# A decoder layer with routed experts: the routing weights' store on another queue, gathers one step earlier, and the first two expert tiles interleaved with shared products

## The chip, the core and the metric

The kernel runs on one core of one Trainium2 chip. TensorE (PE) multiplies; VectorE (DVE), ScalarE (ACT) and GpSimd (POOL) do the elementwise work; SyncE (SP) mostly issues transfers. ACT and POOL can issue transfers too. Each engine works through its own list of instructions in order and waits on semaphores for the others; a transfer counts its semaphore up by 16 when it has landed. The metric is the device time of one execution in microseconds (us).

## What is computed

The layer has three parts: self attention with layer norm, a slot attention with a GRU and layer norm, and a feed forward part with a shared network and eight routed experts, two per token. The change lies in the third:

```python
router_probs = softmax(einsum('bsd,de->bse', x, gate_w) + gate_b)
expert_values, expert_indices = top_k(router_probs, k=2)
expert_values = expert_values / (sum(expert_values) + 1e-09)
h = gelu(einsum('bsd,edi->bsei', x, ew1) + eb1)
all_outputs = einsum('bsei,eid->bsed', h, ew2) + eb2
moe_out = einsum('bse,bsed->bsd', weights_E, all_outputs)   # weights_E: the two values per token
return x + _mlp(x, sh_w1, sh_b1, sh_w2, sh_b2) + moe_out     # then a layer norm
```

There are T = 2048 tokens of D = 256 numbers; the hidden size is I = 1024.

## The kernel before

**Shared network.** The tokens are cut into NG = 4 groups of 512. The hidden units are cut into IC = 8 parts of 128, so there are MS = 32 steps m (group m // 8, part m % 8). A step has an up product (6 matmuls of 512 columns), a gelu and a cast to fp16 on ACT (`hidden`), the low half of the split (value minus its fp16 cast) on POOL (`hidden_low` in `ffn_pool`), and a down product (12 matmuls of 256 columns). Every operand is split in a high and a low fp16 part, which gives three matmuls (`HILO`) for one product. PE takes up(m), then down(m - 2). The first MF = 24 steps run before the experts; the last eight after them, as work for the end.

**Routing**, on DVE beside that: `choose_experts` (two experts per token), `count_tokens` and `place_rows` (where each token's row goes), four `part_choices`, each followed by small matmuls `rows_of` on PE, then `name_rows` (the list `dst` of rows for every tile; semaphore `r_line` reaches `NAMED`) and `name_tiles` (each tile's expert, `TILES_KNOWN`). `weigh_choices` computes the two weights per token, `top_w`; `w_line` counts to 7 when they are there.

**The tokens for the experts** go through DRAM. `store_tokens(k)`, k = 0 to 4, writes them to `rows_x` from five scratch places; two of them (k = 2, 3) are written again by `part_choices`. `store_weights` writes `top_w` beside them, 2048 pieces of 8 bytes, 16 KB. Both are on SP's queue, among 16 loads of 1 MB that bring the experts' weights (`ffn_sync`); `store_weights` comes behind all of these. A row of `rows_x` is a token and its weights.

**Experts.** There are NTILE = 39 tiles of 128 rows. For tile i POOL gathers its rows with an indirect transfer (`gather`), SP turns them with a transposing transfer (`turn_rows`), PE makes the up products (48 matmuls of 128 columns), DVE adds the bias (`biased`), ACT makes gelu and cast (`front`), DVE the low half (`hidden_low` in `experts_vector`), PE the down products (16 matmuls), DVE and ACT scale the result and POOL adds it to `back_y` in DRAM (`scatter`). The expert's weights are addressed by a register. PE takes tiles in pairs: the ups of tile i + 2 dealt out among the downs of tile i (`tile_pair`). The first two tiles have no partner: `tile_pair(0, ...)` and `tile_pair(1, ...)` run up products alone, behind the down products of m = 22 and 23, which the loop of `ffn_tensor` reaches by going on to MF + 2.

**Order by hand.** Gathers 0 and 1 stand in `ffn_pool` behind the low halves of m in `GATHER_AT`; they wait for the row list and for all stores to `rows_x`. SP's order is: weights' store, turn 0, base stores 0 and 1, turns 1 and 2, base store 3, a broadcast of the experts' biases, turn 3, base store 2, turns 4 and on. The base of a group (`shared_out`, `shared_base`) is its shared output plus the tokens, the start value that the experts are added to. PSUM has eight banks: shared ups 0 and 1, shared downs 2 to 5, routing 6 and 7; expert ups 0 to 3, expert downs 4 and 5.

## Time and profile before

| what | us |
|---|---|
| median of 3 runs | 864.14 (863.33 to 867.28) |
| the profiled execution | 863.78 |
| its span (first to last instruction) | 862.5 |
| PE busy | 845.4 |
| DVE busy | 602.3 |
| ACT busy | 548.5 |
| POOL busy | 387.2 |

The profile is of one execution, and times in it count from the start of its span. A row of a timeline gives start, duration, engine, line of the code, operation, tiles written <- read, the count of instructions merged into it, and in brackets the idle time of the engine before it with what ended it. Overlapped matmuls make the duration of a merged row a little longer than the step to the next row.

### The profile page before, as it was taken

The numbers are of one execution on the slowest core, as the hardware profiler recorded it, in microseconds if no ns is written. First come the engines' busy times: TensorE is split into PE (matmuls) and PEld (weight loads), VectorE is DVE, ScalarE is ACT, GpSimd is POOL, SyncE is SP. The second block draws the span as 40 slices with busy tenths as digits, with TensorE's granted clock in tenths as the row PEclk, the third lists the DMA queues.
The fourth block names the chain that finished last, engine by engine and source line by source line (L and its number), as shares of the span: only waits on it lengthen the run. The fifth ranks groups of instructions, "written<-read, shape, count | busy, mean of one in ns | idle before, by whom it ended". The sixth has DMA issues, their size and how long they took to land. (4 is left out here: it accounts for less than half of the span.)

```text
span 862.5 us, 22785 instructions
## 1 busy us (share of the span) xinstructions
PE 845.4 (98%) x8040; PEld 672.9 (78%) x8040; DVE 602.3 (70%) x1638; ACT 548.5 (64%) x1219; POOL 387.2 (45%) x493
## 2 busy tenths in 40 slices
PE   8999999999999999999999999999899999999996
PEld 7888888888888888867666666676688888888864
DVE  6586779776668675756666666888666666666655
ACT  7888877867676776655656655655345555554555
POOL 4543534352433475425534433445535454444433
PEclk9999999999999999999999999999999999999999
DMA  9853424334234333300000000199575555554326
GB/s 314 227 174 121 148 103 144 133 114 148 99 118 128 106 116 58 99 1 2 1 1 1 2 1 1 35 382 370 180 161 79 76 78 78 77 71 87 57 26 201
DMA packets 83626, 93.14 MB, mean 108 GB/s; under 512 B 38559, under 2 KB 69343, under 8 KB 83391
## 3 DMA queue, kind: packets, MB, share of 16 engines
q1 hardware_dynamic: 75487, 80.90, 30.6%
q0 software_dynamic: 7488, 10.27, 8.8%
q8 instruction: 70, 1.15, 0.5%
q10 hardware_dynamic: 544, 0.52, 0.2%
q14 instruction: 37, 0.30, 0.1%
HBM read 56.00 MB, written 30.56 MB: 100 GB/s over the span
## 5 line engine op out<-in xcount | busy, mean ns | idle before, releaser
L667 POOL TENSOR_SCALAR prob<-prob,rden 128x128 f32<-128x128 f32 (+1 forms) x256 | 123.0, 499 | 159.3 <-DVE rden L989 159.3
L2316 PE MATMUL ps<-slots,e 128*128 128x128 f16 x1248 | 124.2, 219 | 0.0
L870 ACT ACTIVATE prob<-prob,nmx 128x128 f32<-128x128 f32 (+1 forms) x256 | 113.2, 446 | 8.6 <-DVE nmx L983 8.6
L2324 PE MATMUL ps<-e,xT 128*128 x312 | 117.2, 379 | 0.0
L2402 ACT ACTIVATE slots<-slots 128x512 f32<-128x512 f32 x78 | 49.1, 630 | 105.8 <-DVE slots L2447 95.0
L2316 PEld LDWEIGHTS ps<-slots,e 128*128 x1248 | 100.9, 97 | 19.1 <-issue 0.2
L2285 POOL DMA_INDIRECT back_y<-xs,dst x39 | 67.5, 1730 | 96.1 <-DMA back_y<-xs,dst 55.2
L983 DVE CUSTOM_DVE_ANT_0 prob<-ps,mask 128x128 f32<-128x128 f32 (+1 forms) x256 | 73.7, 353 | 35.0 <-PE ps L755 34.8
L31 PE MATMUL ps<-xT,wqkv 128*128 128x256 f16 x768 | 94.7, 273 | 0.4 <-ACT slots L877 0.3
L2325 PE MATMUL ps<-e,xT 128*128 x312 | 85.0, 273 | 0.0
L31 PEld LDWEIGHTS ps<-xT,wqkv 128*128 128x128 f16 x768 | 72.1, 98 | 15.3 <-issue 5.9
L2452 DVE TENSOR_TENSOR xT<-slots,xT 128x1024 f16<-128x1024 f32 x39 | 47.8, 1225 | 39.2 <-ACT xT L2408 38.2
L2447 DVE SCALAR_TENSOR_TENSOR slots<-ps,b1e 128x512 f32<-128x512 f32 x78 | 53.8, 692 | 24.7 <-PE ps L2316 22.5
L2316 PE MATMUL ps<-routes,e 128*128 128x128 f16 x624 | 63.9, 219 | 0.2 <-issue 0.2
L877 ACT ACTIVATE slots<-ps 128x512 f32<-128x512 f32 x64 | 37.7, 588 | 37.2 <-PE ps L31 37.2
L593 DVE SCALAR_TENSOR_TENSOR parted<-piece,parted 128x256 f16<-128x256 f32 x144 | 61.0, 471 | 0.0
L2316 PEld LDWEIGHTS ps<-routes,e 128*128 x624 | 51.7, 97 | 10.1 <-issue 0.6
L31 PE MATMUL ps<-an,wqkv 120*128 120x256 f16 x432 | 59.0, 272 | 0.6 <-POOL an L1529 0.6
L31 PEld LDWEIGHTS ps<-an,wqkv 120*128 120x128 f16 x432 | 41.2, 99 | 16.5 <-POOL an L1529 2.6
L31 PE MATMUL ps<-wst,whh 128*128 128x512 f16 x216 | 52.5, 379 | 0.0
L31 PE MATMUL ps<-s,whh 128*128 128x512 f16 x216 | 52.5, 379 | 0.0
L755 PE MATMUL ps<-slots 64*128 64x128 f32 (+1 forms) x512 | 50.9, 338 | 0.0
(279 smaller groups left out, 1897.6 us busy)
## 6 DMA issues: line engine op xcount, KB each, us to landing
halves<-parted SPq DMA_DIRECT2D x36, 512.0 KB, 2.9
piece<-in_L_ffn_ew SPq DMA_DIRECT2D x32, 512.0 KB, 4.5
e<-halves SPq DMA_DIRECT2D x16, 1024.0 KB, 13.8
piece<-in_L_ffn_sh_w SPq DMA_DIRECT2D x4, 512.0 KB, 10.2
sw<-halves SPq DMA_DIRECT2D x4, 512.0 KB, 6.5
xs<-back_y SPq DMA_DIRECT2D x8, 256.0 KB, 5.0
out<-xs SPq DMA_DIRECT2D x8, 256.0 KB, 2.2
xs<-in_x SPq DMA_DIRECT2D x1, 1536.0 KB, 12.5
```

The costliest lines, as they stand in the source:

```text
L31: mm = pe.matmul(out, w, x, start=first and n == 0, stop=last and n == len(products) - 1, **kw)
L593: VE.scalar_tensor_tensor(share(piece_part(q, 1)), share(like_part(q)), WS, share(piece_part(q, 0)), ALU.mult, ALU.subtract).then_inc(p_lo, 1)
L667: PO.tensor_scalar(prob[u][:, h, r], prob[u][:, h, r], rden[u][:, h, t:t + 1], 1.0, ALU.mult, ALU.mult).then_inc(normed, 1)
L755: mm = PE.matmul(ps[:, 2 + 2 * p + h, query_tile(t)], qk[p][r, 0, t * P:t * P + P], qk[p][r, 1, 0:(t + 1) * P], start=True, stop=True)
L870: SC.activation(at, at, ACT.Exp, bias=nmx[u][:, h, t:t + 1], scale=-1.0, accum_out=den[u][:, h, t:t + 1]).then_inc(exped, 1)
L983: VE.tensor_tensor_reduce(prob[u][:, h, r], ps[:, 2 + h, r], mask[:, r], -SCALE, HIGHEST, ALU.add, ALU.min, nmx[u][:, h, t:t + 1]).then_in ...
L2285: PO.indirect_dma_start(back_y, bass.IndirectOffsetOnAxis(ap=dst[:, i:i + 1], axis=0), yo[i % 2], None, compute_op=ALU.add).then_inc(rows_ ...
L2316: yield PE.matmul(ps[:, 2 * u + q, (k % 4) * P:(k % 4) * P + P], w[ch][h], xgT[i % TURNED][:, j * DC + ch, :], start=n == 0, stop=n == 3 * ...
L2324: yield PE.matmul(ps[:, 4 + u, :], he[u][0][:, k, :], w, start=k == 0, stop=False, skip_group_check=True)
L2325: yield PE.matmul(ps[:, 4 + u, 0:D], he[u][1][:, k, :], w[:, 0:D], start=False, stop=k == IC - 1, skip_group_check=True)
L2402: SC.activation(z, z, ACT.Gelu_apprx_tanh).then_inc(U_gelu, 1)
L2447: VE.scalar_tensor_tensor(z, ps[:, 2 * u + q, :].rearrange("p (k t) -> p k t", k=4), 1 / WS, bias, ALU.mult, ALU.add).then_inc(U_bias, 1)
```

## The change

One token store (k = 4) is counted on a semaphore of its own, `stored`; those who need all tokens wait for it as well. The store of the weights goes from SP's queue to ACT's, behind the step m = 17. The weights' computation is cut in two: four operations ahead of `place_rows`, three behind part 1 (`scale_choices`). Gathers 0 and 1 stand one step earlier. The shared downs of m = 22 and 23 are no longer in the loop of `ffn_tensor`; `first_tiles` issues one of their 24 matmuls and then four of the 96 up matmuls of tiles 0 and 1, in turn. PSUM banks are dealt anew for that. On DVE `shared_out(2)` and `shared_base(2)` go behind the first two tiles' hidden parts, and on SP turn 4 goes ahead of base store 2. The diff, with small hunks left out:

```diff
-        TURNED, ROUTED, STORED = 3, 7 * I, 3
+        TURNED, ROUTED, STORED = 3, 7 * I, 2
...
-            GATHER_AT = (20, 21)
+            GATHER_AT = (19, 20)
@@ in store_tokens @@
-                             parts.bitcast(F32)).then_inc(x_early[k] if k < 2 else x_stored, 16)
+                             parts.bitcast(F32)).then_inc((*x_early, x_stored, x_stored, stored)[k], 16)
...
             def store_weights():
-                SY.wait_ge(x_stored, 16 * STORED)
-                SY.wait_ge(w_line, WEIGHED)
-                SY.dma_start(rows_x[P:P + T, D:D + 2].rearrange("(t p) k -> p t k", p=P), top_w,
+                SC.wait_ge(x_stored, 16 * STORED)
+                SC.wait_ge(w_line, WEIGHED)
+                SC.dma_start(rows_x[P:P + T, D:D + 2].rearrange("(t p) k -> p t k", p=P), top_w,
                              allow_slow_non_contiguous=True).then_inc(x_stored, 16)
@@ in ffn_sync @@
-                store_weights()
                 turn_rows(0)
...
                 SY.wait_ge(x_stored, 16 * STORED)
+                SY.wait_ge(stored, 16)
@@ in ffn_pool; the same line also before shared_base(NG - 1) on VE @@
                         PO.wait_ge(x_stored, 16 * (STORED + 1))
+                        PO.wait_ge(stored, 16)
                         gather(GATHER_AT.index(m))
...
-                return m % IC % 2 + (6 if m >= MF else 0)
+                return m % IC % 2 + (2 if m >= MF else 0)
+
+            def up_bank(i):
+
+                return 0 if i % 2 else 6
@@ in up @@
                 if m == MF:
-                    PE.wait_ge(r_line, NAMED)
-                if m == MF + 1:
-                    PE.wait_ge(count_out, 1)
-                    PE.wait_ge(r_line, 20)
+                    PE.wait_ge(O_out, NG - 1)
...
             def down_bank(g):
-                return 4 if g == 1 else 2
+                return (2, 4, 2, 0)[g]
@@ in ffn_tensor @@
-                for m in range(MF + 2):
-                    if m < MF:
-                        up(m)
+                for m in range(MF):
+                    up(m)
@@ in ffn_scalar @@
+                    if m == 17:
+                        store_weights()
@@ in weigh_choices, after its fourth operation @@
+            def scale_choices():
+
                 VE.wait_ge(w_line, 4)
@@ in ffn_vector @@
                     if m == 12:
                         count_tokens()
+                        weigh_choices()
                         place_rows()
                     if m in PART_AT:
                         part_choices(PART_AT.index(m))
                     if m == 14:
-                        weigh_choices()
+                        scale_choices()
...
             def experts_sync():
-                store_base(2)
                 for i in range(4, NTILE):
                     turn_rows(i)
+                    if i == 4:
+                        store_base(2)
@@ in tile_pair @@
-                    if up == 0:
-                        PE.wait_ge(H_gelu, MF)
-                    if up == 1:
-                        PE.wait_ge(O_out, NG - 1)
@@ in experts_tensor @@
+                def first_ups():
+
+                    for i in range(2):
+                        rows_turned(PE, i)
+                        if i == 0:
+                            PE.wait_ge(r_line, NAMED)
+                        else:
+                            PE.wait_ge(H_gelu, MF)
+                        for k in range(IC):
+                            for n, mm in enumerate(up_chunk(i, expert[i], k)):
+                                if k % 4 == 3 and n == 3 * DC - 1:
+                                    mm.then_inc(U_mm, 1)
+                                yield mm
+
+                def last_shared_downs():
+
+                    for m in (MF - 2, MF - 1):
+                        PE.wait_ge(*low_made(m))
+                        PE.wait_ge(H_hi, m + 1)
+                        for t in range(TG):
+                            for n, (i, j) in enumerate(HILO):
+                                mm = PE.matmul(ps[:, down_bank(NG - 2) + t // 2, t % 2 * D:t % 2 * D + D],
+                                               hh[m % 3][i][:, t * P:t * P + P], s2c[j][:, m % IC, :], start=False,
+                                               stop=m == MF - 1 and n == 2, skip_group_check=True)
+                                if t == TG - 1 and n == 2:
+                                    mm.then_inc(O_mm, 1)
+                                yield mm
+
+                def first_tiles():
+
+                    ups, downs = first_ups(), last_shared_downs()
+                    for _ in range(2 * TG * 3):
+                        next(downs)
+                        for _ in itertools.islice(ups, 4):
+                            pass
+                    assert next(ups, None) is None
...
-                tile_pair(0, expert[0], None, None)
-                tile_pair(1, expert[1], None, None)
+                first_tiles()
@@ in experts_vector @@
                 row_weights(0)
                 row_weights(1)
+                biased(0, expert[0])
+                hidden_low(0)
+                row_weights(2)
+                biased(1, expert[1])
+                hidden_low(1)
                 shared_out(2)
-                for i in range(2):
-                    biased(i, expert[i])
-                    hidden_low(i)
-                    if i == 0:
-                        row_weights(2)
-                        shared_base(2)
+                shared_base(2)
```

## Rows read from the trace of the kernel before

**Rows 1.** the page, part 1: busy us, share of the span, instructions
```profile
PE 845.4 (98%) x8040; PEld 672.9 (78%) x8040; DVE 602.3 (70%) x1638; ACT 548.5 (64%) x1219; POOL 387.2 (45%) x493
```

**Rows 2.** waits of PE over the span: us in total, times, longest us
```profile
PE ps L1995 <- DVE slots L2168: 2.8, 2, 2.2
...
PE ps L31 <- POOL slots L1889: 1.5, 1, 1.5
```

**Rows 3.** the chain that ended last, 570 to 640 us: start, us, what
```profile
601.74 10.90 DMA rows_x<-routes
...
619.69 2.79 PE ps L31 x24
622.49 2.91 PE ps L2316 x48
625.39 4.27 PE ps L2316 x48
```

**Rows 4.** timeline of DVE (VectorE): start, us, operation, [idle before <-releaser]
```profile
593.81 1.17 DVE L2161 TENSOR_TENSOR routes<-routes 128x312 f16<-128x312 f32 x1 [0.99 <-DMA rows_x<-xg]
...
599.91 0.96 DVE L2107 TENSOR_TENSOR few<-few 128x16 f32<-128x16 f32 x1
...
622.60 1.23 DVE L2204 SCALAR_TENSOR_TENSOR xT<-ps,b2s 128x1024 f32<-128x1024 f32 x1 [1.33 <-PE ps L31]
...
629.47 1.22 DVE L2222 SCALAR_TENSOR_TENSOR xT<-xs,xT 128x1024 f32<-128x1024 f32 x1
```

**Rows 5.** timeline of PE
```profile
604.60 0.37 PE L1995 MATMUL ps<-slots 128*128 128x39 f16 x8 [2.17 <-DVE slots L2168]
...
612.83 1.46 PE L31 MATMUL ps<-xT,sw 128*128 128x512 f16 x6
614.12 1.47 PE L31 MATMUL ps<-sw,slots 128*128 128x256 f16 x12
...
635.10 0.35 PE L2316 MATMUL ps<-slots,e 128*128 128x128 f16 x3
```

**Rows 6.** timeline of ACT (ScalarE)
```profile
598.99 0.62 ACT L2030 CAST slots<-slots 128x512 f16<-128x512 f32 x1
```

**Rows 7.** DMA packets from 600 to 606, then from 609 to 612 us
```profile
DMA packets 636, 2.46 MB, mean 410 GB/s; under 512 B 36, under 2 KB 36, under 8 KB 636
...
DMA packets 1226, 0.13 MB, mean 44 GB/s; under 512 B 1196, under 2 KB 1196, under 8 KB 1226
```

**Rows 8.** DMA queues from 3.0 to 3.1 us: packets, MB, share of 16 engines
```profile
q1 hardware_dynamic: 15, 0.02, 44.0%
q10 hardware_dynamic: 13, 0.01, 37.4%
```

**Rows 9.** timeline of POOL (GpSimd)
```profile
613.54 1.78 POOL L1792 DMA_INDIRECT xg<-rows_x,dst  x1 [1.86 <-PE ps L31]
615.36 1.17 POOL L1889 TENSOR_TENSOR slots<-slots 128x512 f16<-128x512 f32 x1
616.70 1.76 POOL L1792 DMA_INDIRECT xg<-rows_x,dst  x1 [0.17 <-issue]
...
621.42 1.02 POOL L1792 DMA_INDIRECT slots<-rows_x,dst  x1 [0.17 <-issue]
```

**Rows 10.** timeline of the SyncE queue (SPq)
```profile
620.81 1.41 SPq L1819 DMA_TRANSPOSE slots<-xg  x1
...
626.86 0.50 SPq L1861 DMA_DIRECT2D xs<-in_L_ffn_eb  x1
627.47 1.86 SPq L1819 DMA_TRANSPOSE slots<-xg  x1
```

**Rows 11.** DMA issues from 626 to 640 us: xcount, KB, us to landing
```profile
xs<-in_L_ffn_eb SPq DMA_DIRECT2D x1, 1024.0 KB, 7.4
```

**Rows 12.** PE in stretches at the end: us, busy, granted clock (PEclk), DMA
```profile
855.80:860.30 4.50, 0.00 (x0) 1.00 0.60 200
860.50:862.50 2.00, 0.00 (x0) 0.50 0.80 264
```

More of the change, by code:

```diff
@@ L2216, in shared_base @@
                     VE.wait_ge(x_stored, 16 * STORED)
+                    VE.wait_ge(stored, 16)
                     VE.wait_ge(b_in, 48)
@@ L2310, in up_chunk @@
                 def up_chunk(i, e, k):
-                    u, q = i % 2, k // 4
+                    q = k // 4
                     w = [[e1[:, bass.ds(e, 1), ch, h, k * P:k * P + P].squeeze(1) for h in range(2)]
@@ L2315, in up_chunk @@
                     for n, (ch, (h, j)) in enumerate(itertools.product(range(DC), HILO)):
-                        yield PE.matmul(ps[:, 2 * u + q, (k % 4) * P:(k % 4) * P + P], w[ch][h], xgT[i % TURNED][:, j * DC + ch, :],
+                        yield PE.matmul(ps[:, up_bank(i) + q, (k % 4) * P:(k % 4) * P + P], w[ch][h], xgT[i % TURNED][:, j * DC + ch, :],
                                         start=n == 0, stop=n == 3 * DC - 1)
@@ L2446, in biased @@
                             VE.wait_ge(U_lo, i)
-                        VE.scalar_tensor_tensor(z, ps[:, 2 * u + q, :].rearrange("p (k t) -> p k t", k=4), 1 / WS,
+                        VE.scalar_tensor_tensor(z, ps[:, up_bank(i) + q, :].rearrange("p (k t) -> p k t", k=4), 1 / WS,
                                                 bias, ALU.mult, ALU.add).then_inc(U_bias, 1)
@@ L2519, in combine_sync @@
                     SY.dma_start(ov[:, q * CT:(q + 1) * CT, :], xs[:, q * CT:(q + 1) * CT, :]).then_inc(stored, 16)
-                SY.wait_ge(stored, 16 * CHUNKS)
+                SY.wait_ge(stored, 16 + 16 * CHUNKS)
             def sums(t):
```

## The prediction

> **What bounds the kernel now.** I read the engine shares first: TensorE (PE) is busy for 98% of the span [rows 1]. So only its few idle stretches, or the rate at which it is fed, can be won. Then the waits of PE: in the stretch that the change touches there are three [rows 2]. Two are for the part operands of `rows_of` (0.62 and 2.17 us, together 2.8), one is 1.5 us for the hidden low halves that GpSimd (POOL) makes. Together 4.3 us, which is 0.5% of 864, and 0.5% is about what a measurement of this kernel can tell from no change. Third, the chain: it runs through the 16 KB store of the routing weights, issued at 601.74 and landed 10.9 us later at 612.64, then over POOL's two gathers to the last shared down products, and on through the up products of tiles 0 and 1 [rows 3]. From 629.66 PE runs one pair of expert tiles after another without idling, so what is won or lost at 629.66 is carried to the end. I name that moment H; its counterpart after the change decides everything.
>
> **Earlier parts (all hidden).** The first part choice waits until all token stores have landed, 0.99 us at 593.81 [rows 4]. With one store counted apart it waits for the two whose scratch it overwrites, and they were issued earlier on the same queue; the wait goes. Moving four of the seven weight operations ahead of `place_rows` and leaving three behind part 1 shortens what stands between parts 1 and 2, and the PE wait of 2.17 us ended at 604.60 by exactly that delay [rows 4, 5]. The moved ones can hold `place_rows` back by between nothing and 1 us (one of them took 0.97 us where it met POOL's subtraction [rows 4]). I take 2.5 us of the 2.8 us: PE would end the up product of m = 22 at about 611.6, where before it ended at 614.1 [rows 5].
>
> **Does the store of the weights land sooner?** This is where I chose. Its issue moves from SyncE to ScalarE (ACT) behind the cast of m = 17. That cast began at 598.99 and takes 0.62 us [rows 6], less the 0.6 us that PE gains by then: issued near 599.0, 2.7 us sooner. But the queue was full: from 600 to 606 the 16 DMA engines moved 410 GB/s, 600 packets of the expert weights (4 KB) and 36 small ones, so not one of its 2048 packets of 8 bytes. From 609 to 612 there were 1226 packets, of which 1196 small [rows 7]. The store waits behind the expert loads, and its own packets cost little. On a queue of its own it is served beside them; how? At 3.0 to 3.1 us both hardware queues have work: 15 packets of q1 and 13 of q10 in a tenth of a microsecond, less than two packets for each of 16 engines [rows 8]. So an engine goes from one queue to the other after each packet. Against 4 KB packets that means: the share of one engine is 128 small packets, and a 4 KB packet lasts 16 x 4096 B / 410 GB/s = 0.16 us, so all of them would need 20 us beside the loads. The loads are through before that (about 610.9), and the rest follows them as before. The total is the same, so the landing stays at about 612.6.
>
> The Trainium skill, "DMA: Bandwidth & Descriptors", section "Queues, rings and completion order", says otherwise: an engine drains a whole packet of typically 9 to 17 descriptors, at most 64, before it turns to another row. By that rule, with packets as long as it allows for the small ones, the weights would be through after two or three turns. The row at 3.0 us speaks against it; it has equal sizes, so it isn't proof.
>
> **The gathers.** They move one step ahead, behind POOL's subtractions of m = 19 and 20, and POOL works in order. Since the weights land at 612.6, the first gather still starts at 613.54 [rows 9] (the added wait for the last token store costs nothing, it landed long before). But now the subtraction for m = 20 is queued behind it: 613.54 + 1.78 + 1.17 = 616.5. PE needs it for the down product of m = 20 after 611.6, so PE stands for 4.9 us. Then: down 1.31 and up 1.30 us [rows 5] to 619.2; the subtraction for m = 21 comes behind the second gather (616.70 + 1.75 + 1.17 = 619.6); its down product ends at 620.95; the subtraction for m = 22 ends at 620.8. So the last two down products begin at 621.0, where they began at 619.69: **+1.3 us**. All that was won is waited away, and the gathers come no sooner.
>
> **Interleaving.** From 619.69 to 629.66 there were 9.97 us for 24 down matmuls and 96 up matmuls. At the engine's rates (2.79 us for the 24 downs, 2 x 2.91 for the ups by the first 48 [rows 3]) it would be 8.6. The second 48 took 4.27 us, 0.089 each, with PE shown busy throughout. I read this as the instruction stream: up matmuls take an expert's address from a register and come slower than PE eats them; the first 48 lived on a lead gathered during the long down matmuls. Dealing one down among four ups spends the same instructions, so the same stream time: 96 x 0.089 = 8.5 plus the downs at between nothing and the 2.8 they take on PE, less a lead of about 1.4 (the 4.27 - 2.91 that the first 48 were spared). That is 7.1 to 9.9, and not under the 8.6; I take 9.4, nearest to the 9.97, since no instruction is removed: **-0.6 us**, from -1.4 to 0. The turned rows should be there: tile 1's were used 8.7 us after their gather at the latest (616.70 to 625.39 [rows 3, 9]), which for tile 0 gives 622.2 at the latest against 621.1; I count nothing and keep 1.1 as a bound. H would be at 630.4.
>
> **What is late next.** The turn of tile 3 is issued at 627.47, behind the broadcast of the expert biases (626.86, landing 7.4 us later, 634.3) on the same queue, and tile 3 starts on PE at 635.10 [rows 10, 11, 5]. All of that hangs on gather 2 (621.42), which hangs on the last subtraction [rows 9]. That one now follows the subtraction that ends at 620.8, so it ends at 621.95; before it ended 619.65 + 1.17 = 620.8. Gather 2 starts that much later, near 622.5: +1.1 us, and tile 3's ups with it. So a gain inside the interleaving is taken back here; this end gives +1.1, the sum before gave +0.7. `shared_out(2)` (1.23 us) and `shared_base(2)` (1.22) [rows 4], moved behind the first two tiles on VectorE, stand ahead of the bias of tile 2 with 2.45 us. VectorE is busy for 70% of the span [rows 1], so of a pair's 5.4 us (629.66 to 635.10) some 1.6 are free: 0 to 0.8 once, and I take 0, because the chain of gather 2 covers it. SyncE's turn 4 passes `store_base(2)`: off the path. Banks change no duration.
>
> **Sum.** -2.5 (waits won) + 2.5 (waited again) + 1.3 - 0.6, or by the chain of gather 2 +1.1: **+1.0 us**, bounds +0.3 and +1.6. The profiled run took 863.78 (span 862.5 and 1.3 around it); the median shown is 864.14, from which I count: **865.1**.
>
> **Rivals.**
> - *The clock falls (slower).* PE idles 4.9 us in one piece. At the end of the span PE stood still from 855.8 on: the granted clock was full (2.4 GHz) through a stretch of 4.5 us and half (1.2 GHz) after 860.5 [rows 12]. The stretch ahead is just longer, so it can fall. From then on PE needs double time; between 616.5 and 621.0 it has 1.31 + 1.30 + 1.31 = 3.9 us of work and 0.5 us of slack. If all of it is at half, +3.4; if only the first two products, +2.1. On top of +1.0: 867 to 868.5. For it: the length. Against: nothing between 2.2 us (no fall in this stretch [rows 2]) and 4.5 tells where it begins.
> - *The weights land early (faster).* If an engine serves long bunches of small packets, the store lands by 605 and nothing waits. POOL then keeps pace, the down products of m = 22 begin at about 615.8, and the interleaving ends at 625.2. But gather 2 starts no sooner than after the last subtraction (about 617.7), 3.7 us ahead of 621.42, and tile 3 follows it: -3.7 us, 860.4. If landing is at 609, the subtraction for m = 22 ends 8.2 us later, 617.2: -2.3, 861.8. It decides between 607.5 (full gain) and 612.
> - *The second half of the change comes out at the engine's rates*, with the landing late: H at 621.0 + 8.6 = 629.6, no change against before, but tile 3 still comes at +1.1; so it can't show.
>
> **Chances.** Forecast +1.0: 0.52. Clock falls, +3: 0.22. Early landing (whole or in part), -4.7 to -2: 0.20. Others 0.06. The range takes in both rivals' middle: 860.5 to 868.0. The likeliest case alone: 864.4 to 865.8. Faster by over 0.5% (under 859.8) needs the whole 4.7 us: 0.06. Slower by over 0.5% (over 868.5) needs the fallen clock at its worst: 0.10. Within: 0.84.
>
> **What would show it.** Right: in the changed profile the ACT-issued store lands at 612 to 613; POOL idles before the first gather; PE has one wait of 4 to 5 us for POOL's subtraction and none for `rows_of`; 120 matmuls in 9 to 10 us. Wrong: a landing before 608 moves the first gather to about 608 and H under 626; PEclk under 1 after 616 is the clock rival; 120 matmuls in 8.6 us or less refutes the instruction stream.

## The result and the profile after

The changed kernel takes 866.08 us (median; 864.22 to 867.87) where the kernel before takes 863.79 in the same series: a ratio of 1.0027 (95% interval 1.002 to 1.0034), that is 2.3 us slower. Its profiled execution took 865.91, of which the span is 864.6. The forecast was 865.1. PE is busy for about as long as before (845.4 us in [rows 1]), so the 2.1 us by which the span is longer are idle time. A slower clock hides in the busy time, and so does what the interleaving saved:

```profile
PE 845.0 (98%) x8040; PEld 671.3 (78%) x8040; DVE 603.8 (70%) x1638; ACT 548.3 (63%) x1219; POOL 386.6 (45%) x493
```

The waits of PE in the changed kernel (us in total, times, longest; compare [rows 2]):

```profile
PE ps L31 <- POOL slots L1889: 3.6, 1, 3.6
PE ps L2325 <- DVE xT L2493: 2.1, 2, 1.4
```

The 2.8 us for the part operands are down to 0.4 (0.39, in the first row of the next view). In their place stands one wait of 3.6 for a subtraction on POOL. Further on there are two waits for low halves that DVE makes, together 2.1 us: 1.35 at 631.28 for tile 0's, and 0.71 at 642.83 for tile 2's. The timeline of PE in the changed kernel shows them in order (compare [rows 5]):

```profile
601.84 0.37 PE L1997 MATMUL ps<-slots 128*128 128x39 f16 x8 [0.39 <-DVE slots L2174]
...
610.27 1.46 PE L31 MATMUL ps<-xT,sw 128*128 128x512 f16 x6
615.32 1.80 PE L31 MATMUL ps<-sw,slots 128*128 128x256 f16 x12 [3.59 <-POOL slots L1889]
616.91 2.77 PE L31 MATMUL ps<-xT,sw 128*128 128x512 f16 x6
619.47 1.62 PE L31 MATMUL ps<-sw,slots 128*128 128x256 f16 x12
620.92 0.27 PE L2382 MATMUL ps<-sw,slots 128*128 128x256 f16 x1
621.03 0.39 PE L2325 MATMUL ps<-slots,e 128*128 128x128 f16 x4
621.26 0.27 PE L2382 MATMUL ps<-sw,slots 128*128 128x256 f16 x1
```

The up product of m = 22 ends at 611.73, where 611.6 was forecast. The products after the wait are stretched: an up product that takes 1.46 us takes 2.77. The reason is the clock; PE in stretches of the changed kernel (us, busy and matmuls, granted clock, DMA share, GB/s):

```profile
611.80:615.20 3.40, 0.00 (x0) 1.00 0.12 27
615.40:616.20 0.80, 0.80 (x8) 1.00 0.00 0
616.40:619.60 3.20, 3.20 (x11) 0.50 0.74 206
```

PE stands still under a full clock, works 0.8 us under it, and is then granted half (1.2 of 2.4 GHz) for about 3.4 us, from 616.3 to 619.75. The last rows are from POOL's timeline of the changed kernel (compare [rows 9]):

```profile
611.87 2.20 POOL L1792 DMA_INDIRECT xg<-rows_x,dst  x1 [5.76 <-DMA rows_x<-routes]
614.10 1.16 POOL L1889 TENSOR_TENSOR slots<-slots 128x512 f16<-128x512 f32 x1
615.43 0.96 POOL L1792 DMA_INDIRECT xg<-rows_x,dst  x1 [0.17 <-issue]
616.40 2.27 POOL L1889 TENSOR_TENSOR slots<-slots 128x512 f16<-128x512 f32 x2
621.13 1.16 POOL L1889 TENSOR_TENSOR slots<-slots 128x512 f16<-128x512 f32 x1 [2.45 <-ACT slots L2031]
```

POOL idles 5.76 us in front of the first gather, with the subtraction that PE needs queued behind it.

To compare executions, which differ by a few tenths in their early parts (`first_half` by 1.0), I shift each so that the down product of m = 13 stands where it stands in the trace of before. All times below called aligned are of that kind, and agree to about 0.02 us. The shift of the changed kernel is +0.41 us, so its up product of m = 22 ends at 612.14 on the scale of the kernel before, 0.5 later than forecast. Positions are from PE's timelines; "pair n" is the start of the first 512-column matmul of the pair whose downs are those of tile n.

| aligned, us | before | changed | changed, second execution |
|---|---|---|---|
| downs of m = 22 begin | 619.70 | 621.34 | 621.64 |
| pair 0 | 629.91 | 631.94 | 630.25 |
| pair 1 | 635.34 | 637.26 | 639.13 |
| pair 2 | 640.69 | 643.49 | 646.07 |

### The profile page after: what moved, and what is told of

It reads as the page before. It is cut to its first block and busy times, and to the rows that moved or that the text cites. A ratio compares the mean times of both kernels' runs of the same rounds, so it can differ in the third digit from the quotient of the medians.

```text
span 864.6 us, 22785 instructions
## 1 busy us (share of the span) xinstructions
PE 845.0 (98%) x8040; PEld 671.3 (78%) x8040; DVE 603.8 (70%) x1638; ACT 548.3 (63%) x1219; POOL 386.6 (45%) x493
## 5 line engine op out<-in xcount | busy, mean ns | idle before, releaser
L2325 PEld LDWEIGHTS ps<-slots,e 128*128 x1248 | 102.8, 97 | 20.2 <-issue 1.6
```

What stands on the lines that cost most here:

```text
L2325: yield PE.matmul(ps[:, up_bank(i) + q, (k % 4) * P:(k % 4) * P + P], w[ch][h], xgT[i % TURNED][:, j * DC + ch, :], start=n == 0, stop=n = ...
```

## The experiments

All medians are in us; each ratio is against the kernel before, measured on the same chip at the same time (medians 863.51 for the first four kernels, 863.4 for the next four, 862.78 for the last four). The ratio is an estimate of its own and can differ from the quotient of the two medians by up to 0.0009: `turn_first` is 4.0 us faster by medians and 3.3 by its ratio, `second_half` 1.1 slower by medians and 1.7 by its ratio.

| kernel | median | ratio (95%) |
|---|---|---|
| first_half | 866.09 | 1.0022 (1.0013 to 1.0032) |
| second_half | 864.59 | 1.002 (1.0007 to 1.0033) |
| gathers_back | 864.2 | 1.0008 (0.9998 to 1.0019) |
| filler | 865.89 | 1.003 (1.0021 to 1.004) |
| store_sync | 867.47 | 1.0038 (1.0025 to 1.0051) |
| store_early | 861.11 | 0.9966 (0.9947 to 0.9985) |
| vector_order | 865.81 | 1.0031 (1.0014 to 1.0048) |
| spaced | 866.83 | 1.0034 (1.002 to 1.0048) |
| changed_again | 865.53 | 1.003 (1.0017 to 1.0043) |
| turn_first | 858.75 | 0.9962 (0.9948 to 0.9976) |
| turn_first_vector | 858.65 | 0.9958 (0.9945 to 0.9972) |
| no_dealing | 860.13 | 0.9972 (0.9962 to 0.9983) |

### Which half of the change costs the time

`first_half` keeps the stores, the weights' order and the earlier gathers, and takes the interleaving, the banks and the two reorderings on DVE and SP back. `second_half` is the other half alone. The edit of `first_half`, in its main lines:

```diff
-                first_tiles()
+                tile_pair(0, expert[0], None, None)
+                tile_pair(1, expert[1], None, None)
```

The edit of `second_half`, against the changed kernel, in its main lines:

```diff
-            GATHER_AT = (19, 20)
+            GATHER_AT = (20, 21)
...
-                SC.dma_start(rows_x[P:P + T, D:D + 2].rearrange("(t p) k -> p t k", p=P), top_w,
+                SY.dma_start(rows_x[P:P + T, D:D + 2].rearrange("(t p) k -> p t k", p=P), top_w,
```

> The kernel before with the first half of the change alone: one token store counted apart, the weights' store on ScalarE's queue, the weights' computation cut in two, gathers one step earlier. No interleaving, no new banks, VectorE's and SyncE's order as before. Theory 1 (the gathers queue GpSimd's low half behind a store that lands no sooner): TensorE stands 3.5 to 5 us for the low half of m = 20, the last two shared downs begin within 1.7 us of where they began before (in the changed kernel's profile 620.9 against 619.7), the up products of tile 1 take 4.3 us as before: 0 to +1.7 us. Theory 2 (the loss of the change lies in its second half): the first half alone is a gain, at least -1 us, because the 2.8 us of waits for rows_of are gone.

> The changed kernel with the first half undone: only the first two tiles' ups dealt out among the last shared downs, the new banks, VectorE's order (shared_out(2), shared_base(2) behind the two tiles) and SyncE's (turn 4 before base store 2). Theory 1: the last two shared downs begin as before, the 120 matmuls take 8.9 to 9.4 us instead of 9.97, tile 0's bias comes late and VectorE's two moved operations hold back tile 2: together -0.5 to +0.5 us. Theory 2 (the second half carries the loss): +1.5 us or more.

`first_half` has the wait of 3.58 us and the half clock after it (3.4 us from 617.5 on), starts the downs of m = 22 at 621.34 aligned (+1.6) and is slower by 1.0022 (1.9 us, or 2.6 by medians, where 0 to 1.7 was expected). `second_half` has neither, starts them at 619.74 (+0.0), reaches pair 2 at 640.86 (+0.2), and is still slower by 1.002. That lies between its two theories (at most +0.5, at least +1.5) and settles neither. For that second figure its profile shows no place: the profiled execution took 863.58, about what the one of before took. Neither half is a gain. What stays in the dark of `second_half` is why its median is a microsecond above its profile.

### The gathers' place against POOL's subtractions

```diff
-            GATHER_AT = (19, 20)
+            GATHER_AT = (20, 21)
```

> The changed kernel with the gathers back at their old step (20, 21), all else as changed. Theory 1: the low half of m = 20 is made in time, the one stand of 3.6 us becomes two of at most 1.5 us, the granted clock stays full, and the last two shared downs begin 2 to 3 us sooner than in the changed kernel: -2 to -3 us against it, so 0 to -1 us against the kernel before. Theory 2 (the place of the gathers doesn't matter, since they wait for the same landing either way): within 0.5 us of the changed kernel, +2.3 us against before.

With the rest of the change in place, the wait of 3.6 us becomes these (PE's timeline of `gathers_back`):

```profile
615.56 1.48 PE L31 MATMUL ps<-sw,slots 128*128 128x256 f16 x12 [0.82 <-POOL slots L1889]
617.93 0.27 PE L2382 MATMUL ps<-sw,slots 128*128 128x256 f16 x1 [0.88 <-issue]
619.41 0.46 PE L2325 MATMUL ps<-slots,e 128*128 128x128 f16 x4 [1.22 <-DMA slots<-xg]
...
635.88 0.35 PE L2325 MATMUL ps<-slots,e 128*128 128x128 f16 x3 [1.16 <-DMA slots<-xg]
```

The downs of m = 22 begin at 618.08 aligned, 3.3 us ahead of the changed kernel. The turned rows are now what is late, for tile 0 (1.22) and for tile 3 (1.16), and what arrives in the time is the ratio of 1.0008 in place of 1.0027 and 1.003, 1.6 to 1.9 us and not the 2 to 3 expected. The clock didn't stay full either: it was at half from 620.1 to 623.5. So moving the gathers one step forward is what costs most, as the prediction had it; they can't start before the weights are there, and everything queued behind them waits.

### Does the fallen clock cost anything?

`filler` puts 14 matmuls of 512 columns in front of the down product of m = 20, into a bank that is free then. Their results are read by nobody; nothing else is changed.

```diff
+                    if m == MF - 2:
+                        PE.wait_ge(O_out, 2)
+                        for n in range(14):
+                            PE.matmul(ps[:, 4, :], s1c[0][:, 0, 0:P], s1c[0][:, 0, 0:GT], start=True, stop=True)
```

> The changed kernel with 14 more matmuls of 512 columns on TensorE (3.0 us, their result is overwritten and read by nobody) between the up product of m = 22 and the down product of m = 20, so that TensorE stands less than 1 us there. Theory 1 (the granted clock falls because TensorE stands for 3.6 us): the clock stays at 1.0, the products behind the wait take 1.3 us each instead of 2.8 and 1.6, and the kernel is 1 to 1.7 us faster than the changed one although it does more. Theory 2 (the clock in the profile fell by chance, or its fall is hidden by later waits): no difference, within 0.4 us.

The matmuls fill 611.86 to 615.05, PE waits 0.56, and the clock stays full (PE in stretches of `filler`):

```profile
615.00:616.40 1.40, 0.84 (x9) 1.00 0.35 94
616.40:619.60 3.20, 3.20 (x26) 1.00 0.63 169
```

The downs of m = 22 begin at 619.66 aligned, where before they began at 619.70 and in the changed kernel at 621.34. So the half clock costs 1.68 us at this place, as the rows say too: from 615.32 to 620.92 PE takes 5.60 us for work that takes 1.31 + 1.30 + 1.31 = 3.92 at full clock. Yet the median is 865.89, that of the changed kernel. In the profiled execution pair 2 begins 1.2 us ahead of the changed kernel's (642.25 against 643.48 aligned), but the span is 0.7 longer: 0.86 us are given back waiting for the turn of tile 3, and 1.33 at the very end (timelines of PE, `filler`, then changed):

```profile
636.55 0.35 PE L2329 MATMUL ps<-slots,e 128*128 128x128 f16 x3 [0.86 <-DMA slots<-xg]
...
853.90 1.97 PE L2408 MATMUL ps<-xs,routes 128*128 128x256 f32 x8 [1.33 <-DMA xs<-back_y]
```

```profile
853.54 1.97 PE L2404 MATMUL ps<-xs,routes 128*128 128x256 f32 x8 [0.20 <-DMA xs<-back_y]
```

So this fall is real and of the size named, but taking it away wins no time. The first of the two waits has a cause that other runs show (below); that the wait at the end follows from the edit is not shown. A second fall, behind the wait for tile 3's turn, is another matter, as told there.

### The store's queue, and its place in the queue

`store_sync` puts the weights' store back where it was, behind all loads on SP. `store_early` puts it on SP ahead of the last two 1 MB loads. The edit of `store_early` (that of `store_sync` has the call behind the loop over the loads):

```diff
+                        if (e, k) == (E - 1, 0):
+                            store_weights()
...
-                    if m == 17:
-                        store_weights()
```

> The changed kernel with the weights' store back on SyncE's queue behind all loads. Theory 1 (beside 4 KB packets the small ones get one turn each, so both queues give the same landing): it lands at 610.5 to 612.5 as in the changed kernel, time within 0.4 us. Theory 2 (ScalarE's queue brings it forward): it lands 1 us or more later, and the kernel is slower by as much.

> The changed kernel with the weights' store on SyncE's queue, ahead of the last two loads of expert weights instead of behind all of them; the last loads are issued some 8 us later. Theory 1 (the gathers are set by the store's landing, and that by what is ahead of it in the queue): the store lands at 606 to 608 instead of 611.0, the first gather starts by 608.5, TensorE's stand before the down product of m = 20 shrinks from 3.6 us to under 1 us without a fall of the clock, and the first pair of tiles begins 3 to 4.5 us sooner: -3 to -4 us against the changed kernel, -1 to -2 against before. Theory 2 (the store takes its 11 us wherever it stands): it lands at 611 or later, within 0.5 us of the changed kernel. Theory 3 (the loads, issued late, land after 615 and now hold up the first expert tiles): slower than the changed kernel.

On ACT's queue the store is issued at 599.95 and lands at 610.98, 11.0 us later (the issues of the changed kernel from 600 to 603: count, size, us to landing):

```profile
rows_x<-routes ACTq DMA_DIRECT2D x1, 16.0 KB, 11.0
```

The last load lands at 610.01, just before it. In `store_sync` the last load lands at 610.79 and the store at 612.17, 1.4 us behind. In the trace of before it was 611.28 (where the prediction had about 610.9) and 612.64, 1.4 behind as well. The other profiles say the same: on ACT's queue the store lands 0.95 to 1.0 us behind the last load (seven profiles), behind the loads on SP's 1.3 to 1.4 (three, with `second_half`). So the queue brings 0.4 us relative to the loads. The end of the loads varies more than that, from 610.4 to 611.5 aligned between two executions of the changed kernel. In the time, 1.0038 against 1.0027 and 1.003, the two can't be told apart for sure. How the two queues share is plain in one microsecond of the changed kernel, 604 to 605 (packets and MB of each queue, with its share of the 16 engines):

```profile
DMA packets 207, 0.41 MB, mean 406 GB/s; under 512 B 108, under 2 KB 108, under 8 KB 207
...
q1 hardware_dynamic: 104, 0.41, 98.7%
q10 hardware_dynamic: 103, 0.00, 5.8%
```

104 packets of 4 KB (a few of 4 bytes among them), 103 of 8 bytes: one for one. Equal counts could also come from equal bunches, so the single starts matter: from 604 to 606 a 4 KB packet starts 5 to 7 ns after the start of a small one for 194 of 207 small ones, which is one engine taking one from each queue in turn. The Trainium skill, "DMA: Bandwidth & Descriptors", section "Queues, rings and completion order", has an engine drain typically 9 to 17 descriptors, at most 64, before it turns; this trace doesn't agree, and the measurement decides.

With the store ahead of two loads, POOL is no longer short of work (its timeline in `store_early`):

```profile
608.63 1.26 POOL L1792 DMA_INDIRECT xg<-rows_x,dst  x1 [1.95 <-DVE routes L2200]
609.91 1.16 POOL L1891 TENSOR_TENSOR slots<-slots 128x512 f16<-128x512 f32 x1
```

The store lands at 607.74, the first gather now waits for the row list (`DVE routes`) and no longer for the weights, the wait of 3.6 us is gone, the clock stays full up to 634.5, and the downs of m = 22 begin at 616.64 aligned, 4.7 us ahead of the changed kernel. The time goes to 861.11. In the profiled execution 4.1 us are then waited away in one piece, and the clock falls behind it (PE's timeline of `store_early`, then PE in a stretch):

```profile
635.12 0.50 PE L2325 MATMUL ps<-slots,e 128*128 128x128 f16 x3 [4.15 <-DMA slots<-xg]
```

```profile
634.80:637.80 3.00, 2.68 (x18) 0.50 0.78 194
```

This execution took 864.01, the slowest of the eight; they reach down to 859.08. So this loss need not occur in each of them; the others have no profile.

### What ends the first gather

The store landed at 611.39 and at 612.42 aligned in the two executions of the changed kernel, 1.0 us apart, and PE waited 3.59 us in both. What holds the gather back besides the landing is VectorE. POOL's timeline of `changed_again` (compare the first two rows of POOL's timeline in the section on the result), and DVE's of the changed kernel's first execution:

```profile
612.88 1.46 POOL L1792 DMA_INDIRECT xg<-rows_x,dst  x1 [6.49 <-DMA rows_x<-routes]
614.37 1.16 POOL L1889 TENSOR_TENSOR slots<-slots 128x512 f16<-128x512 f32 x1
```

```profile
611.73 1.22 DVE L2225 SCALAR_TENSOR_TENSOR xs<-xs,b2s 128x1024 f32<-128x1024 f32 x1
```

The first gather took 2.20 us when it began at 611.87, and 1.46 when it began at 612.88. In the first execution it ended 1.12 us after this DVE operation (612.95, then 614.07), in the second too (613.21, then 614.33). The same 1.12 or 1.13 us lie between the end of the DVE operation that ran when the gather began and the end of the gather in all ten profiles in which one ran, those of the kernel before and of `second_half` among them. Where none ran (`store_early`, `turn_first`, `turn_first_vector`, `no_dealing`) the first gather took 1.25 to 1.29 us. So between about 611.4 and 612.4 the landing hardly mattered. No run moves the DVE operation by itself.

### Tile 3's turn, and the executions in which it is late

The same wait appears without that edit. `changed_again` is the changed kernel once more.

> The changed kernel once more, for a second profile. Theory 1 (the stand of 3.6 us for the low half of m = 20 comes from the order of the work, the fall of the clock behind it from the stand): both are there again, as in first_half, spaced, vector_order and store_sync. Whether TensorE's counts come 2.3 us late, as in three of seven profiles, or in time, is open: if late again, it belongs to this kernel; if in time, it differs from one execution to the next. Time +1.8 to +2.8 us against before.

Its PE timeline (the wait of 3.6 us and the half clock are there again, the counts come in time):

```profile
615.58 2.40 PE L31 MATMUL ps<-sw,slots 128*128 128x256 f16 x12 [3.59 <-POOL slots L1889]
...
638.38 0.35 PE L2325 MATMUL ps<-slots,e 128*128 128x128 f16 x3 [3.31 <-DMA slots<-xg]
```

Here pair 0 comes 1.7 us sooner than in the first execution (630.25 against 631.94) and pair 1 1.9 later. The first execution lost its time on another way: tile 0's up products were finished at about 625.0, but DVE, which adds the bias, was released at 627.31 only. DVE's timeline in both, first the changed kernel's first execution:

```profile
623.24 0.69 DVE L2488 SCALAR_TENSOR_TENSOR slots<-ps,b1e 128x512 f32<-128x512 f32 x1 [3.96 <-issue]
627.45 0.69 DVE L2488 SCALAR_TENSOR_TENSOR slots<-ps,b1e 128x512 f32<-128x512 f32 x1 [3.51 <-remote]
```

```profile
623.50 0.69 DVE L2488 SCALAR_TENSOR_TENSOR slots<-ps,b1e 128x512 f32<-128x512 f32 x1 [3.96 <-PE ps L2325]
625.49 0.69 DVE L2488 SCALAR_TENSOR_TENSOR slots<-ps,b1e 128x512 f32<-128x512 f32 x1 [1.29 <-PE ps L2325]
```

PE's counts came about 2.3 us late in the first, and in `first_half` and `filler`. In the other profiles they came in time, but for one count in `second_half`, about 1.5 us late, which nobody waited for. I suspected the three gathers in a row that POOL issues at 622.97, 624.29 and 625.54. `spaced` holds the third back until tile 0's ups are counted:

```diff
+                            if i == 4:
+                                PO.wait_ge(U_mm, 2)
```

> The changed kernel with one wait more: GpSimd starts gather 4 only when the ups of tile 0 are counted as done. In the profiles so far TensorE's counts come late, all at once, 1.7 us after the start of the last of the gathers 2, 3, 4 that GpSimd issues without a pause (in the changed kernel tile 0's ups are done at 625.0 by their matmuls and counted at 627.3). Theory 1 (three gathers in a row hold TensorE's counts back): the count comes by 625.8, VectorE's bias for tile 0 with it, TensorE doesn't wait 1.4 us for tile 0's low half, -1 to -1.5 us against the changed kernel, so +0.8 to +1.3 against before. Theory 2 (the delay belongs to the interleaving or to TensorE's own instruction stream): the count stays 2 us late and the time within 0.4 us of the changed kernel.

`vector_order` gives DVE its old order, with the shared output and base of group 2 behind tile 2's bias instead of ahead of it:

```diff
-                shared_out(2)
-                shared_base(2)
                 for i in range(NTILE):
...
+                    if i == 0:
+                        shared_out(2)
+                        shared_base(2)
```

> The changed kernel with shared_out(2) and shared_base(2) on VectorE moved again, from behind the first two tiles' low halves to behind the bias of tile 2. Theory 1 (those 2.45 us ahead of the bias of tile 2 make TensorE wait 0.7 us for that tile's low half): the wait goes, -0.5 to -0.9 us. Theory 2 (the bias of tile 2 was held back by the rows, not by the two operations, or the wait comes back one step later): within 0.3 us of the changed kernel.

`spaced` has the counts in time and is no faster (1.0034), so its theory 1 fails in the time. And `vector_order` and `store_sync` have them in time too with the three gathers in a row as they were, so the gathers aren't the cause; it differs from execution to execution and stays open. What both say is that it doesn't matter for the time: with counts in time, PE waits 3.16 us (`spaced`), 2.68 (`vector_order`) and 3.74 (`store_sync`) for tile 3's turn instead. `vector_order` removes the wait for tile 2's low half and gains nothing, since that later wait takes it up. So in these executions the end of the stretch is set by the turn of tile 3. In the changed kernel's first execution it isn't: there the turn landed at 635.07, tile 3 was taken up at 636.65 without a wait, and what was lost are the 1.35 and 0.71 us for DVE.

The wait also brings a second fall of the clock. In `changed_again` it was at half from 639.9 to 643.3, right behind the wait, and from pair 1 to pair 2 PE took 6.94 us where before it took 5.35. `vector_order`, `spaced` and `store_early` have this fall too; `store_sync`, with 3.74 us of waiting, doesn't. With these 1.6 us pair 2 stands at +5.4 in the table (646.07); at the end of the span +4.0 is left. SP's timeline in `changed_again`, and the chain that leads through it:

```profile
628.57 0.45 SPq L1861 DMA_DIRECT2D xs<-in_L_ffn_eb  x1
629.13 3.33 SPq L1819 DMA_TRANSPOSE slots<-xg  x2
```

```profile
623.32 3.32 DMA slots<-rows_x,dst
629.13 9.01 DMA slots<-xg
```

The turn is issued right behind the 1 MB broadcast of the expert biases [rows 10, 11], and lands 9.0 us later; in `store_early`, 11.1. Wherever the broadcast was issued first the turn landed behind it, by 0.6 to 3.2 us. But the broadcast isn't its only neighbour: in SP's new order the turn of tile 4 is issued right behind it. With the old order the turn took 7.4 us (kernel before) and 6.1 (`first_half`); with the new one 6.3 and 6.6 in two profiles and 8.0 to 11.1 in seven.

### Turning first

`turn_first` is `store_early` with one more exchange, tile 3's turn ahead of the broadcast. `turn_first_vector` adds to it the order on DVE of `vector_order`. `no_dealing` is `turn_first` without the interleaving: tiles 0 and 1 are multiplied alone behind all the shared downs, as before, and with that the banks and the order of DVE and of SP's base store 2 are the old ones.

```diff
                 store_base(NG - 1)
+                turn_rows(3)
                 SY.wait_ge(x_stored, 16 * STORED)
                 SY.wait_ge(stored, 16)
                 SY.dma_start(b2e, a["L0_ffn_eb2"].rearrange("(o e) d -> o e d", o=1).broadcast_to(
                     (P, E, D))).then_inc(b2e_in, 16)
-                turn_rows(3)
```

> store_early (the changed kernel with the weights' store ahead of the last two expert loads) with one more exchange on SyncE's queue: turn 3 ahead of the broadcast of the expert biases. In store_early the first pair of tiles began 4.1 us sooner than in the kernel before, and then TensorE stood 4.15 us for tile 3, whose turn was issued behind that 1 MB broadcast. Theory 1 (the broadcast ahead of it in the queue is what makes turn 3 late): turn 3 lands before 630, TensorE goes on without a stand at tile 3, the clock stays full until the end, and the kernel is 4 to 5.5 us faster than before. Theory 2 (turn 3 is late for another reason: the gathers, or transposing beside them): it still lands after 633 and the time is that of store_early, -2 to -3 us. Theory 3 (the broadcast becomes late and holds the result of tile 0 and its scatter): the wait moves there, -2 to -3 us.

> turn_first with shared_out(2) and shared_base(2) behind the bias of tile 2 on VectorE, as in vector_order. Theory 1 (the two operations cost TensorE 0.7 to 1.1 us at tile 2's downs once the turn no longer hides them): 0.5 to 1 us faster than turn_first. Theory 2: no difference over 0.3 us.

> The first half of the change with the same two exchanges on SyncE's queue as turn_first (store ahead of the last two loads, turn 3 ahead of the broadcast), but without the dealing out of the first tiles' ups, without the new banks and with VectorE's and SyncE's old order otherwise. Theory 1 (dealing out is worth the 1 us by which its 120 matmuls are shorter, 8.8 against 9.97 us, and turn 0 must be there sooner for it): 0.5 to 1.5 us slower than turn_first, still 3 us faster than before. Theory 2 (dealing out gains nothing, because the first tile's low half is late in either order): within 0.3 us of turn_first_vector.

The wait for the turn is gone; between 598 and 650 us PE has these two waits in `turn_first`, and the clock is full from 610 to 640:

```profile
602.09 0.37 PE L1999 MATMUL ps<-slots 128*128 128x39 f16 x8 [0.38 <-DVE slots L2174]
...
624.77 0.37 PE L2325 MATMUL ps<-routes,e 128*128 128x128 f16 x3 [0.77 <-issue]
```

```profile
610.00:640.00 30.00, 29.23 (x343) 1.00 0.76 195
```

Its SP timeline has the turn in front:

```profile
623.42 1.61 SPq L1819 DMA_TRANSPOSE slots<-xg  x1
625.13 0.53 SPq L1864 DMA_DIRECT2D xs<-in_L_ffn_eb  x1
```

It lands at 627.15 aligned instead of 634.99 in `store_early`, 3.6 us after its issue, and pair 2 stands at 635.95, 4.7 us ahead of before and 7.5 ahead of the changed kernel. The exchange takes the turn away from in front of turn 4 as well as from behind the broadcast, so which of the two made it late isn't shown. The median is 858.75, 4.0 under the kernel before (3.3 by the ratio): the fastest version here, together with `turn_first_vector`, which is the same within its interval. What the exchange adds to `store_early` in the time is less sure: 1.7 us by the medians against their kernels before, 0.3 by the ratios, whose intervals overlap. Here, without a later wait to take it up, DVE's order costs nothing either. `no_dealing` is 1.4 us slower than `turn_first` and has PE busy throughout the up products:

```profile
618.07 1.48 PE L31 MATMUL ps<-sw,slots 128*128 128x256 f16 x12 [0.56 <-POOL slots L1891]
619.39 7.54 PE L2324 MATMUL ps<-slots,e 128*128 128x128 f16 x96
```

96 up matmuls alone take 7.54 us, 0.079 each, where the first 48 of [rows 3] took 0.061. Dealt among the downs, the changed kernel steps 0.33 us from one down to the next with four ups between (620.92, 621.26). With 0.11 for the down (1.31 us for 12) that leaves 0.056 for each up. It holds for the first 15 rounds in its first execution, and in `changed_again` for all 24, which take 8.0 us.

## Why the prediction was right, and where it was not

**The waits won (-2.5).** Right, a little too high. 2.8 us of waits went to 0.4, and up(22) began 2.15 us sooner (610.68 aligned against 612.83).

**The store doesn't land sooner by its queue.** Right, by the mechanism given: packets go one for one. It landed 1.2 us sooner in the first execution all the same (611.39 aligned instead of 612.64): 0.4 by the queue, and 0.8 since all loads ended sooner (610.01, aligned 610.42, against 611.28). The second execution had only the 0.4 of the queue, less a loss of 0.2 (612.42), so the 0.8 doesn't belong to the change; why executions differ in it is open.

**The gathers hold the subtraction back.** Right as a mechanism, and `gathers_back` isolates it: 1.6 to 1.9 us of the time. The size was off: PE stood for 3.6 us and not 4.9. Of the 1.3 us, 0.5 are PE's later arrival (612.14 aligned and not 611.6). The other 0.8 are the end of the subtraction, 615.67 aligned where 616.5 was forecast. I had added the gather's 1.78 us of the kernel before to its start, but its end goes by DVE's operation beside it, and that ended sooner here. The landing doesn't explain it: in the second execution it came at 612.42, near the forecast, and the wait was the same.

**The last downs at +1.3.** Measured +1.64, but for another reason, and this is the step that failed. At full clock the shorter wait gives 615.32 + 3.92 = 619.24, aligned 619.66, or +0.0 (`filler` shows that 619.66). The 1.68 us on top are the half clock, which I had put among the rivals at 0.22. It happened in all six profiles with a wait of 3.6 to 3.7 us at this place, and at this place in none of the eight others (`gathers_back` had it later, from 620.1). Two errors cancelled: a way to the last downs that was 1.3 too long (0.8 of it the late subtraction, 0.4 a wait for the next subtraction that didn't come), and a clock left out. That +1.3 and +1.64 lie close together is luck. The rival's result, +2.1 to +3.4 on top, was wrong as well: the fall cost 1.68 us at this place, and `filler` shows that even these don't reach the end. The second fall, behind tile 3's turn, no rival had.

**Interleaving (-0.6, bounds -1.4 to 0).** Too small. The changed kernel took about 8.84 us for the 120 matmuls in its first execution (620.92 to 629.76) and 8.0 in its second, where before took 9.97: -1.1 and -2.0. That is also under the 8.6 that I had as the engine's rate and as a floor; it was worked out from 0.061 per up matmul, and they go at 0.056. With nothing else in the way, about 1.4 us reach the median (`no_dealing` against `turn_first`). I had taken the stream's 0.089 us per up matmul as spent in any order. That the ups alone are fed too slowly held (0.079 each), but dealt out they came at 0.056. My reading is that the stream catches up while a down matmul, whose address is fixed, runs for its 0.11 us; no run tests that reason. The sign I had named, that 8.6 us or less would refute the stream, was a wrong one: `turn_first` took 8.3 for the 120 matmuls, and `no_dealing` shows the slow stream nonetheless.

**What is late next: tile 3's turn, +1.1.** Right in name for every profile but the first, in which the turn came in time. The last subtraction waits 2.45 us for the cast of m = 23, which is itself behind the half clock, so gather 2 came at +2.0 aligned and not +1.1. And the landing isn't gather 2 plus a fixed time: from gather to landing it was 13.4 us before (621.42 to 634.86), 12.1 in the changed kernel's first execution and 14.8 in the second (623.32 to 638.14). SP issues the turns of tiles 3 and 4 back to back in the new order; I had called that off the path. Turn 3 took 8.0 us or more only in that order, but not always in it; whether turn 4 makes it slower was not tried by itself.

**DVE's two operations ahead of tile 2's bias (0 to 0.8, I took 0).** Right for the time: `vector_order` and `turn_first_vector` show no difference. In the changed kernel's first execution they cost PE 0.71 us (the wait for tile 2's low half).

**Sum.** +1.0 was forecast, +2.3 measured. (The terms as written give +0.7 by one way and +1.1 by the other; +1.0 was a choice between them.) The kind of loss was right: what is won in front is waited away at POOL, then at the turn. The gain by dealing doesn't show in the time of the changed kernel. The missing 1.3 us lie behind the dealing, but not in one term: pair 1 stood at +1.9 in the first profile, by the late counts, and DVE's wait made it +2.8 at pair 2; in the second it stood at +3.8 by the turn, and the half clock made it +5.4. At the end of the span the two are at +2.5 and +4.0 (the spans are 864.6 and 866.1 against 862.5, and the shifts of 0.4 come on top).

**The rival of the early landing** was refuted for the changed kernel and true as a mechanism: brought about by order instead of by queue, the landing at 606.6 to 607.7 gives what it said (POOL keeps pace, downs of m = 22 at 615.88 to 616.64 where it had 615.8). But it had tile 3 follow gather 2 with -3.7; with the turn behind the broadcast -2.3 us came in the median (-2.9 by the ratio), and with the turn in front -4.0 (-3.3).

## What to carry to other kernels

Before giving a transfer a queue of its own, ask what it shares its engines with: here 2048 tiny packets went one for one beside a full stream of large ones and landed 1.0 us behind it, which was worth 0.4 us; a place ahead of two loads in the same queue made it land 3.5 us or more sooner. Before moving an instruction that waits for a transfer forward on an in-order engine, read what will stand behind it. After each wait that is taken away look for the next one on the list, here a transpose issued between a 1 MB broadcast and another transpose, since what is won in front is given back there. And one profile is one execution: two of this kernel lost their time at different places.

## What the runs showed of the hardware that was not expected

PE's clock was granted at half for 3.4 us (6.8 in `store_sync` and `vector_order`) around the end of an idle wait of 3.6 to 3.7 us. It fell between 1.0 us before PE took up work again (`vector_order`, at 614.7) and 1.0 us after (the changed kernel, 616.3), so the wait's length alone doesn't give the moment. In `gathers_back` it fell too, at 620.1, after waits of only 0.82, 0.88 and 1.22 us. And in `store_sync` it did not fall at the wait of 3.74 us for tile 3's turn, where `vector_order` had a fall at 2.68.

A DVE operation on one number per partition took 2.86 us while POOL ran three instructions in a row, and ended with the last of them (DVE's timeline of the changed kernel; the second row is the same operation for the next tile):

```profile
615.84 2.86 DVE L2475 TENSOR_TENSOR mask<-xg,mask 128x1 f32<-128x1 f32 x1 [2.89 <-DMA xg<-rows_x,dst]
...
618.87 0.15 DVE L2475 TENSOR_TENSOR mask<-xg,mask 128x1 f32<-128x1 f32 x1
```

POOL's subtractions stood at 616.40 to 618.67. Eight profiles have it, with 2.78 to 2.86 us. It was off the critical path here; no run isolates it. Its mirror image, the first gather that ends 1.12 us after a DVE operation, was on the path.

Semaphore counts of PE reached DVE 2.3 us after the work in one execution of the changed kernel and in time in the other. The cause is open.
